# Adaptive-norm model with two layers on one core: the second attention's first batch is prepared in the experts' last chunk, and two fills move

## What is computed

```python
h = _layernorm(x) * (1 + cb) + sb                 # layer 0, experts
x = x + gb * experts(h, controller, f1, bias, f2)
# layer 1, attention
h = _layernorm(x) * (1 + ca) + sa
q, k, v = split_heads(h @ Wq + bq), split_heads(h @ Wk + bk), split_heads(h @ Wv + bv)
q, k = _rope(q), _rope(k)                          # 16 heads of 8
probs = softmax(q @ k.T / sqrt(8))
x = x + ga * ((probs @ v) @ Wo + bo)
```

## Time and profile before

| | us |
|---|---|
| three runs, median | 1354.55 |
| three runs, lowest and highest | 1353.51, 1354.78 |
| the profiled execution | 1355.31 |
| its span | 1353.5 |
| TensorE busy in the span | 1219.1 (90%) |
| VectorE busy | 1063.2 (79%) |
| ScalarE busy | 925.2 (68%) |
| GpSimd busy | 537.6 (40%) |

### The profile page before, as it was taken

One profiled execution on the slowest core, in us unless ns is written; L12 is line 12 of the kernel. 1 busy time (PEld: TensorE's weight loads), 2 busy tenths in 40 slices (PEclk: granted clock), 3 DMA queues, 4 the chain that ended last, 5 costly groups with the idle time before them and its releaser, 6 DMA issues. The chain is left out here.

```text
span 1353.5 us, 39636 instructions
## 1 busy us (share of the span) xinstructions
PE 1219.1 (90%) x13671; PEld 808.1 (60%) x13671; DVE 1063.2 (79%) x2968; ACT 925.2 (68%) x1280; POOL 537.6 (40%) x743
## 2 busy tenths in 40 slices
PE   2699999999996899985899999999669999999998
PEld 1455555555553677773555555555347878787776
DVE  3799999999965788755899999999357777777763
ACT  0388888888893555541787888787637666767665
POOL 1333333333321232213334333344335565656553
PEclk7699999999998999997899999999869999999999
DMA  3411111111001111102000000000000000000000
GB/s 91 157 38 36 35 35 35 35 35 35 27 10 47 43 35 31 27 18 95 12 15 12 16 12 15 12 12 16 3 1 1 16 15 8 15 8 15 8 15 25
DMA packets 44749, 37.80 MB, mean 28 GB/s; under 512 B 5008, under 2 KB 43472, under 8 KB 44144
## 3 DMA queue, kind: packets, MB, share of 16 engines
q1 hardware_dynamic: 44656, 36.56, 9.8%
HBM read 32.21 MB, written 4.34 MB: 27 GB/s over the span
## 5 line engine op out<-in xcount | busy, mean ns | idle before, releaser
L2111 ACT ACTIVATE a_probs<-psum_all 128x1024 f32<-128x1024 f32 x256 | 248.2, 1022 | 86.5 <-PE psum_all L2026 86.4
L562 ACT ACTIVATE probs<-psum_all,biases 128x1024 f32<-128x1024 f32 x256 | 272.5, 1112 | 37.7 <-PE psum_all L473 36.2
L2457 PE MATMUL psum_all<-ffn_hi,weights_r 128*128 128x512 f32 x704 | 285.9, 406 | 8.7 <-POOL ffn_lo L2417 5.3
L2457 PE MATMUL psum_all<-ffn_lo,weights_r 128*128 128x512 f32 x704 | 279.7, 397 | 0.0
L2417 POOL TENSOR_TENSOR ffn_lo<-ffn_full,ffn_hi 128x512 fp32r<-128x512 f32 x144 | 188.8, 1319 | 126.6 <-ACT ffn_hi L2542 86.8
L2457 PEld LDWEIGHTS psum_all<-ffn_hi,weights_r 128*128 128x128 f32 x704 | 134.2, 191 | 50.2 <-DVE ffn_full L2672 9.5
L2457 PEld LDWEIGHTS psum_all<-ffn_lo,weights_r 128*128 128x128 f32 x704 | 134.7, 191 | 26.6
L2040 PE MATMUL psum_all<-a_probs,vpad 128*32 128x256 f32 x2048 | 137.5, 386 | 2.3 <-DVE a_sums L2264 2.3
L486 PE MATMUL psum_all<-probs,vpad 128*32 128x257 f32 x2048 | 138.0, 387 | 0.7 <-ACT probs L562 0.3
L2554 ACT ACTIVATE ffn_full<-psum_all,scales 128x512 f32<-128x512 f32 x128 | 88.2, 689 | 68.9 <-PE psum_all L2457 68.7
L2417 DVE TENSOR_TENSOR ffn_lo<-ffn_full,ffn_hi 128x512 fp32r<-128x512 f32 x64 | 55.3, 864 | 79.8 <-ACT ffn_hi L2557 79.8
(11 more groups left out here) (226 smaller groups left out, 2628.8 us busy)
## 6 DMA issues: line engine op xcount, KB each, us to landing
a_mod_gate<-modulation_table SPq DMA_DIRECT2D x64, 128.0 KB, 2.9
X<-in_x SPq DMA_DIRECT2D x32, 128.0 KB, 2.9
a_mod_norm<-modulation_table SPq DMA_DIRECT2D x32, 128.0 KB, 3.0
f<-in_f SPq DMA_DIRECT2D x2, 2048.0 KB, 10.1
e_mod_norm<-modulation_table SPq DMA_DIRECT2D x32, 128.0 KB, 2.9
out<-X SPq DMA_DIRECT2D x16, 256.0 KB, 2.3
e_gates<-modulation_table SPq DMA_DIRECT2D x32, 64.0 KB, 2.9
weights<-in_h SPq DMA_DIRECT2D x2, 1024.0 KB, 7.5
```

Of the source, the lines that this page charges most:

```text
L562: nc.scalar.activation(probs[:, c % 4, :, :, 0:T].rearrange("p r k q -> p (r k) q"), SC[c % 2].rearrange("p (a q) -> p a q", q=T), ACT.Tan ...
L2111: nc.scalar.activation(probs[:, c % 4, :, :, :].rearrange("p r k q -> p (r k q)"), SC[c % 2], ACT.Exp, scale=float(np.float32(1.0) / np.sq ...
L2457: ins = nc.tensor.matmul(dst, weights[:, w0:w0 + P], part[layer][:, k, :], start=first and i == 0, stop=last and i == len(parts) - 1)
```

## The change

A new function `attention_1_opening` holds the buffers, semaphores and steps of the attention that run up to the stacks, taken over word for word from the bounded program; it is built ahead of the experts, and both use it. `experts_0` takes it as `following` and issues these steps in its last chunk:

```diff
             # TensorE
+                if m == NCHUNK - 1:
+                    if s == 4:
+                        following["turn"](pe, 0)
+                    if s == 5:
+                        following["project_qk"](pe, 0, 0)
+                    if s == 6:
+                        following["turn"](pe, 1)
                 if i in HALVED:
                     send_half(i, 0)
...
             # GpSimd, at the end of a step
+                if m == NCHUNK - 1:
+                    if s == 2:
+                        following["norm"](pool, 0)
+                    if s == 4:
+                        following["norm"](pool, 1)
+                    if s == 5:
+                        following["rotate"](pool, 0)
...
             # VectorE, between the two copies of a step
+                if m == NCHUNK - 1:
+                    if s == 4:
+                        following["norm_a"](dve, 1)
+                    if s == 5:
+                        following["norm_b"](dve, 1)
+                    if s == 6:
+                        following["cosines"](dve, 0)
+                    if s == 7:
+                        following["high"](dve, 0, 0)
...
             # VectorE, at the end of a step
+                if m == NCHUNK - 1:
+                    if s == 2:
+                        following["norm_a"](dve, 0)
+                    if s == 3:
+                        following["norm_b"](dve, 0)
+                    if s == 4:
+                        following["turned_out"](dve, 0, 0)
+                    if s == 5:
+                        following["add_biases"](dve, 0)
+                    if s == 6:
+                        following["rotated"](dve, 0)
+            following["low"](dve, 0, 0)
```

```diff
     def every(eng, step):
-        stepped(eng, -3, B + 1, 4, 12, step)
+        stepped(eng, -1, B + 1, 4, 12, step)
...
             if there(b + 2):
-                rotate(b + 2)
+                opening["rotate"](pool, b + 2)
+            if isinstance(b, int) and b == -1:
+                padding(1)
             if there(b):
                 gate(b, p)
...
+        def padding(i):
+            v = vpad[i]
+            nc.gpsimd.memset(v[:, :, :, :], 0.0).then_inc(zeroed, 1)
+            pool.wait_ge(zeroed, i + 1)
+
+            for a in range(2):
+                last = nc.gpsimd.memset(v[:, :, a:H:2, 16 * a + HD:16 * a + HD + 1], 1.0)
+            last.then_inc(ones_done, 1)
+
+        padding(0)
         every(pool, step)
...
         def values(n, p):
             dve.wait_ge(v_psum, n + 1)
+            if isinstance(n, int) and n < 2:
+                dve.wait_ge(ones_done, n + 1)
...
-def attention_1_setup(nc, ctx, dram, sbuf, psum):
...
-                with ExitStack() as first:
-                    attention_1_setup(nc, first, dram, sbuf, psum)
```

277 lines of the change are left out of this document (149 added, 128 removed).

## The result

| | before | changed |
|---|---|---|
| median of the runs, us | 1354.03 (four: 1352.98 to 1354.78) | 1341.6 (four: 1340.35 to 1342.28) |
| the profiled execution, us | 1355.31 (span 1353.5) | 1341.68 (span 1339.9) |
| ScalarE's first exponential of the second attention | 648.83 | 635.92 |
| VectorE's first operation of the feed-forward net | 984.84 | 971.96 |
| the last addition to `X` | 1350.07 | 1336.45 |

The ratio is 0.9902, with a 95% interval of 0.9888 to 0.9916: 12.4 us between the medians. The forecast was 1343.0 us and the range 1339.6 to 1346.8; the first exponential was expected near 637.2 and came at 635.92.

A forecast was written before the change was run, and what follows sets the result against it. The handover was taken as latency-bound, one chain of small dependent steps. 11.19 + 2.79 - 0.9 - 0.1 - 1.3 - 0.1 = 11.6 us off the median 1354.55 gave 1343.0 us, range 1339.6 to 1346.8.

The forecast's parts named there:

- Steps taken out, 11.19: Handover to the second attention: attention steps -3 and -2 leave the latency chain, a gain of 11.19 us.
- The block taken out, 2.79: Between experts and attention: without the setup block, the entry takes 1.31 instead of 4.10 us, a gain of 2.79.
- rival B: Attention's entry: an engine is late through the branch, costing up to 1.9 us, 1344.9 us; chance 0.08.
- TensorE in the tail, 0.9: Experts' last chunk: `project_qk` exceeds its wait by 0.6 us, the first `turn` by 0.3 at low clock; 0.9 lost.
- VectorE in the tail, 0.1: Experts' last chunk: VectorE's added operations nearly fit its idle times, 0.1 us lost, bounds 0 to 0.6.
- The low halves, 1.3: Behind the last gate: two subtractions and GpSimd's last residual exclude each other, 1.3 us lost; 0.57 if not.
- The fills, 0.1: Attention's program: the fills moved there are nearly hidden on GpSimd, 0.1 us lost, bounds 0 to 1.0.
- A, the clock at another place: Tail and opening: TensorE's clock rises or falls elsewhere, 1340.5 us if earlier, 1345.3 if later; chance 0.14.
- C: Second attention: its batches settle into a period 0.47 us longer over 31 intervals, 1357.5 us; chance 0.02.
- D, the tail does not hide: Experts' last chunk: every added VectorE and TensorE operation lands on the chain, 1349.5 us; chance 0.05.

The follow-up runs named there:

- after_again: The changed kernel without an edit, profiled and timed again; median 1343.21 us of six runs, ratio 0.991 to the kernel before.
- opening_alone: The changed kernel with the setup block and its fills put back between experts and attention, the opening still in the experts' last chunk; 1345.79 us, ratio 0.9929.
- fills_alone: The changed kernel with nothing issued early in the experts' last chunk, attention from step -3, fills still in the attention's program; 1352.92 us, ratio 0.9976.
- low_split: The changed kernel with the key half of the two `low` subtractions issued ahead of the last gate, the query half behind it; 1344.62 us, ratio 0.9916.
- bridged: The changed kernel with unread TensorE matmuls over the handover, eight behind the experts' last hand-back and two at the attention's start; 1342.79 us, ratio 0.99.
- project_twice: The changed kernel with `project_qk` in step 5 of the experts' last chunk issued twice over the same place; 1343.85 us, ratio 0.9914.
- together: The changed kernel with unread matmuls before step 4, at the handover and in attention step -1, low_split's edit, and `vpad_1` zeros before batch 1's rotation; 1340.34 us, ratio 0.9873.

## Why the prediction was right, and where its terms were off

**Steps taken out, 11.19:** right. From VectorE's first operation of the attention to batch 2's `a_hT` it is 20.37 before and 9.17 after, 11.20 less, and to the last `a_hT` 307.53 before and 296.28 after (296.64 in after_again), 11.25 less (10.89). The opening brings it and not the fills: 296.78 in opening_alone, 307.57 in fills_alone.

**The block taken out, 2.79:** 2.43 came. The new entry took 1.67 and not 1.31. fills_alone, with the same single handover, took 1.34, and opening_alone 1.33 behind its last fill. SyncE issues its first DMA 1.17 us behind the last work in the kernel before and in the changed one; VectorE is the one that is later.

The trace has the place, in the instructions that an engine's sequencer (the part that waits, loads registers and branches) handles alone. In the changed kernel VectorE passes the barrier at the experts' end at 625.03, with SyncE (625.02), but begins the load of the flag only at 625.48, 0.45 behind it, and SyncE at 625.10, 0.08 behind. In fills_alone VectorE needs 0.09 (624.20, 624.29). opening_alone has the delay too: VectorE passes the barrier at 626.20 and begins its next instruction at 626.70, where the kernel before has 624.33 and 624.48; there the fills of GpSimd cover it. So the 0.34 comes with the opening in the experts' last chunk and shows once the fills no longer hide it. The order in which the engines arrive does not make it: in low_split VectorE is done at 633.07, ahead of GpSimd's residual (633.65), and loses the same 0.44 behind the barrier. What holds VectorE there was not found. It is rival B in a small size, on another engine than TensorE.

The Trainium skill ("Runtime: NRT & Kernel Launch", section "Instruction fetch mechanics") says that a taken branch to code that is not fetched stalls the engine. TensorE, for which the prediction allowed up to 1.9 us of this, shows none (in bridged its first matmul of the attention starts at 627.35, 0.31 ahead of VectorE's first operation); whether VectorE's 0.34 is such a stall no run here shows.

**TensorE in the tail, 0.9:** 0.30. Two sizes were wrong in `project_qk`: 0.97 was taken where TensorE is held 0.87, and the idle time of 0.35 where 0.51 was free. The 0.97 was from start to start, but at another place: at 660.28 the first of its four matmul records holds TensorE 0.32 us and the other three 0.22 each, and in the tail, behind the transposes, all four hold it 0.22. And the 0.3 for the first `turn` at the low clock did not come: with the low clock the tail was 19.09 (after_again) against 18.77 to 18.82 with the old tail, 0.3 more, which is `project_qk` alone, and from the first transposes to the first even gate, with the `turn` between, it was 4.51 against 4.54. The rule "what exceeds the idle time is paid in full" held: project_twice paid 0.86 for 0.87.

**VectorE in the tail, 0.1:** nothing that can be seen. All even gates behind step 5 stay 4.33 apart, with the normalization, the cosines, the sum and the casts between them. The cosines took 1.22 us beside GpSimd's `rotate` (615.13) instead of 0.68, and still no gate moved. Ahead of step 4, where the first normalization lies, nothing shows either: from the "issue" row of the first matrices to the first transposes it is 11.92 and 12.19 in the two executions before and 12.09 in both of the changed kernel. (618.54 and 622.87, which the prediction calls even gates, are odd ones; the period is 4.33 for both kinds.)

**The low halves, 1.3:** 0.93 (the experts end at 624.82 for a last gate at 622.67, 2.15; before 624.09 for 622.87, 1.22). The mechanism was the one taken: the two engines exclude each other. GpSimd's residual takes 1.10 instead of 0.72 and the second subtraction 1.21 instead of 0.68, though they overlap in the records. The size was wrong because records were added end to end: a subtraction starts 0.60 behind the one before it (623.01, 623.61) and not 0.69, the first starts 0.08 before the gate's record ends, and the residual held the second subtraction for 0.53 and not for its own 0.72.

That fits the rule of the Trainium skill ("SBUF — State Buffer", section "Who interferes with whom") that one of the two blocks for the whole of the other: residual 0.38 longer, subtraction 0.53 longer. In low_split a normalization of VectorE waited out a fill by GpSimd, which only writes (1.53 us, and VectorE went on 0.07 behind the fill's end). The same section of the Trainium skill has that case for copies, casts and scaling operations of VectorE that take both ports, whoever issues first going first. The trace agrees on the waiting, but not plainly on the order: the record of the normalization begins 4.57 us behind VectorE's first operation and that of the fill 5.07, both while GpSimd's rotation still ran (to 5.12), and yet the fill went first.

**The fills, 0.1:** nothing in the ordinary order, 0.69 in one execution of low_split; the bound of 1.0 was the right one to keep.

**The sum.** With the measured terms it is 11.19 + 2.43 - 0.30 - 0.93 = 12.4, against 11.6 in the prediction and 12.4 between the medians. That the last two agree to the tenth is luck: the interval of the ratio is 1.9 us to either side. So is part of the prediction's closeness, since its terms erred both ways: the entry was 0.36 worse than forecast, and the other four terms 0.6, 0.4, 0.1 and 0.1 better. The forecast of 1343.0 is 1.4 above the measured 1341.6, 0.8 of it from the terms and 0.5 from the median it started at (1354.55, now 1354.03). The first exponential of the profiles moved 12.91: 12.4, and 0.5 net of chance, the clock that did not fall in step 4 (some 1.3) less the longer waits ahead of it (step 4 began 604.88 - 604.05 = 0.83 later).

**Rivals.** A, the clock at another place: in the opening it came back where the prediction left it, at 652.7 before and at 640.1 in the changed kernel, 13.3 and 13.6 us behind batch 1's `a_hT`. Elsewhere the mechanism is real, but as scatter between executions of one kernel (1.3 us in step 4, up to 2.4 in the attention's last batches, 6 in the second matrices once), and only bridged and together turn it into a gain. B: not on TensorE; 0.34 on VectorE, with the place known and the cause open. C: batch intervals are 9.69 and 10.04 by turns in all kernels, to 0.01; it fell. D, the tail does not hide: it hid all but 0.30 and the subtractions; it fell.

## What to carry to other kernels

Here, issuing the next stage's latency chain inside the idle gaps of the previous stage paid the whole length of the chain, because nearly every piece was put in front of a wait that it fits in; what exceeded the wait was paid almost to the full. Take the room and the piece from start to start of neighbouring instructions, not from record lengths, which overlap, and take the piece where its neighbours are like those of its new place. Measure a saving at the chain that feeds the pipeline and at the last batch, not at the first output of the busiest engine, which can be moved by 1.4 us for nothing.

## What was not expected of the hardware

The granted clock falls at different places in executions of one and the same kernel, and that alone makes some per mille of the time: the attention's last batches, with identical instructions, took 47.9 to 50.4 us, and in the changed kernel it was 49.19 once and 47.94 the next time. In the profile with 47.94 the clock was 0.50 from 936 to 939, in that with 49.19 it was 0.75 and 0.68 from 939 to 945, where TensorE had more to do (busy 2.80 and 3.00 of each 3 us, and 0.89 from 936 to 939). Matmuls whose results nobody reads, put into waits of TensorE, kept the clock at 1.00 over 40 us without lengthening any of the marks (together).

A wait of TensorE marked "issue" stands in the middle of one run of 256 matmuls in every profile, at the same instruction, and takes 0.82 to 1.52 us, in the kernel before as in the changed one.
